# The head of a token model's kernel: K loads of group 0 moved to GpSimd, batch 1's norm moved up, a semaphore per gathered tile, memsets moved to the front

## The chip, the cores and the metric

The kernel runs on one core of one Trainium2 chip. The metric is the device time of one execution in microseconds (us). The engines are TensorE (PE; its weight loads are shown as PEld), VectorE (DVE), ScalarE (ACT), GpSimd (POOL) and SyncE (SP), which only issues DMAs here. Each works through its own instruction stream in order and waits on semaphores.

## The reference

The input is 4 batches of 512 token ids. Three stages follow each other, all in float32 (C = 192 channels).

```python
h = LN(concat_h table_h[(id + 1) * prime_h % 4096]) * scale + bias     # 8 tables of 24 columns
x = layernorm(h)                                                       # attention, 12 heads of 16
q, k, v = split(x @ qkv_w.T + qkv_b)
out = softmax(q k^T / 4) v ; out = out @ proj_w.T + proj_b
u = out / |out| per head ; sim = 10 u u^T, where < 0: -inf
h = h + (softmax(sim) v) @ proj_w.T + proj_b
x = layernorm(h)                                                       # 8 experts, the best 2 of each token
h = h + sum_k weight_k * (gelu(x @ w1[e_k] + b1) @ w2[e_k] + b2)
```

## The kernel before, in words

Tokens lie on the 128 partitions, 16 tiles of 128 tokens in all, four (`CT`) for each of the 4 batches (`B`). GpSimd gathers the 16 tiles of embeddings into `H` by indirect DMAs, one for each tile (line 743), and each batch has one semaphore, `gathered[b]`, that counts its four.

For each batch there follow: `embed_norm` (five parts: statistics, moments and centring on VectorE, `rstd` as a logarithm and an exponential on ScalarE, and `affine` on VectorE, which first refines the root by three small instructions), `attn_stats` (the same statistics once more, on the result, with its own `rstd` on ScalarE), and `attn_norm`, which refines that root and writes the normalised tokens `X`. TensorE transposes `X` (`x_transpose`, line 1515), ScalarE copies that to `XT`, and TensorE makes q, k and a third projection c (`q_proj`, `k_proj`, `c_proj`, line 1526; c holds the q and k of the third group of a batch) and v (`v_proj`, line 1534).

Scores are made in bf16 with float32's accuracy: each of q, k and c is split in three bf16 parts, H, M and L. ScalarE copies H from PSUM (line 889), TensorE subtracts it in PSUM (line 1481), ScalarE copies M (line 861), TensorE subtracts it, and ScalarE copies L (line 864). SyncE and GpSimd then copy the parts by DMA into stacks of 96 rows, `QS` and `KS`, so that one matmul of 96 rows adds six products of parts (`load_part`, line 627; the DMA is on line 634, and in the trace `KS` of the first pass is named late_stacks, all else of the kind arena). There are 12 groups, three for each batch, of four heads; a group needs six Q copies and six K copies of 64 KB. SyncE issues all Q copies; it also issues the K copies of group 0, alternating with the Q copies (lines 687 to 691). GpSimd issues the K copies of all other groups. Before ScalarE overwrites the parts of q, k or c with the next batch's, it waits until all copies of them have landed (`wait_stack`, line 637).

A group goes through 16 units of scores for its row maxima (`max_unit`: TensorE line 1542, VectorE reduces each, line 1258), then 16 units of exponentials (`exp_unit`: TensorE line 1550, ScalarE line 908; two rows more of the stack hold minus the maximum, and ones on K's side), products with v (line 1470), and a second pass of the same form on the similarity of the outputs (line 1557). Last comes the routing and the expert layer (lines 1607 to 1650), which works on the slots of tokens in a loop of its own.

The order of the work is one list, `EVENTS`: `schedule` makes the events of each kind in order, and `PLACE` gives each kind its places in the list. Every engine runs through the same list and takes what is its own. So a place decides between which of its other instructions an engine does the work; PSUM banks come from the string `BANKS` in the order of the units that need one. Around the head, the list before is:

```text
0-6   batch 0: stats, moments, centre, rstd, affine, attn stats, attn moments     7  batch 1: stats
8, 9  batch 0: attn rstd, attn_norm     10, 11 x_transpose 0     12 q_proj 0     13 load 0
14    batch 1: moments     15 k_proj 0     16 load 1     17 mid q     18, 19 loads 2, 3     20 batch 1: centre
21, 22 loads 4, 5     23 batch 1: rstd     24 low q     25 mid k     26-28 batch 1: affine, attn stats, attn moments
29    batch 2: stats     30 batch 1: attn rstd     31 v_proj 0 (first half)     32, 34 loads of group 1     33 low k
35    batch 1: attn_norm     36-38 batch 2: moments, centre, rstd     39 c_proj 0     40, 41 x_transpose 1
42    v_proj 0 (second half)     43 mid c     44 ... max_unit
```

GpSimd's stream begins with the identity matrix, the 16 gathers, four memsets of ones into `KS` (line 749; two rows of each of the four stacks), and the constants of the routing (lines 752 to 771). Only then come its loads. VectorE clears the two accumulators in PSUM and sets the ones columns of `V` right after `attn_norm` of batch 0 (lines 1247 to 1251).

## Time and profile before

| what | us |
|---|---|
| median of 3 runs (567.55 to 568.56) | 568.02 |
| the profiled execution | 566.18 |
| its span in the trace | 564.4 |
| TensorE busy | 513.6 (91%) |
| VectorE busy | 402.0 (71%) |
| ScalarE busy | 351.3 (62%) |
| GpSimd busy | 204.8 (36%) |

The span is the trace's own length, from the first instruction to the last; the profiled execution's time has 1.8 us around it. Mean granted clock of TensorE is 0.981 of full speed. The busy time of an engine counts its work, not its DMA issues' waits; a row "SPq" or "POOLq" is the queue that issues. In the chain of waits each step is followed back to what released it, so its shares tell on what the end hangs.

### The profile page before, as it was taken

To read this page: it belongs to the slowest core of one execution; us is meant where nothing else is said; L and a number is where in the kernel's file an instruction comes from. 1 tells how busy PE (TensorE), PEld (TensorE's weight loads), DVE (VectorE), ACT (ScalarE), POOL (GpSimd) and SP (SyncE) were. 2 spreads that over 40 slices of the span, in tenths; PEclk is the share of its full clock that TensorE was granted. 3 is DMA by queue.
4 is the path that set the end of the run, shared out by engine and by line. 5 is a ranking of instruction groups with operands and counts; after the bars stand their busy time and mean duration, and the time that the engine had idled before them with its cause. 6 is when DMAs were issued, how large, how long until landed. Compare 5 with 4: busy or idle time off the path is not lost.

```text
span 564.4 us, 11981 instructions
## 1 busy us (share of the span) xinstructions
PE 513.6 (91%) x3542; PEld 322.7 (57%) x3543; DVE 402.0 (71%) x895; ACT 351.3 (62%) x830; POOL 204.8 (36%) x260
## 2 busy tenths in 40 slices
PE   0469999999999999999999999689989999999990
PEld 0244334543353433545364443479979999999990
DVE  2659999898989999998579999477764343443420
ACT  1134796788898888989989989353323344243330
POOL 6873040235042140102221220223555666666542
PEclk9989999999999999999999999889999999999996
DMA  6266051348061241104334469792232333333322
GB/s 118 63 110 88 29 101 15 57 65 130 33 104 43 64 85 48 58 1 122 57 58 112 67 177 277 206 323 47 42 49 45 57 60 49 49 50 55 41 29 21
DMA packets 42539, 45.23 MB, mean 80 GB/s; under 512 B 10419, under 2 KB 37429, under 8 KB 42486
## 3 DMA queue, kind: packets, MB, share of 16 engines
q0 software_dynamic: 12672, 19.58, 20.2%
q1 hardware_dynamic: 29814, 25.01, 18.8%
q8 instruction: 26, 0.43, 0.4%
q14 instruction: 27, 0.22, 0.2%
HBM read 17.88 MB, written 7.70 MB: 45 GB/s over the span
## 4 chain that ended last, share of the span: by engine, by line
PE 79%; issue 7%; DVE 5%; ACT 4%; DMA 2%; DVEq 1%; POOL 0%; POOLq 0%; SPq 0%; ACTq 0%
PE psum L1470 15%; PE psum L1630 12%; PE psum L1550 8%; PE psum L1607 8%; PE psum L1542 7%; PE psum L1557 7%; PE psum L1614 4%; PE psum L1579 4%; PE psum L1526 3%; PE psum L1515 3%; PE psum L1568 2%; PE psum L1534 2%; DMA result<-T,slot_dest 2%; ACT arena L908 1%; PE psum L1481 1%
## 5 line engine op out<-in xcount | busy, mean ns | idle before, releaser
L908 ACT ACTIVATE arena<-psum 128x512 f32<-128x512 f32 x384 | 203.6, 630 | 17.2 <-PE psum L1550 8.1
L1258 DVE TENSOR_REDUCE MX<-psum 128x1 f32<-128x512 f32 x192 | 121.2, 682 | 13.3 <-PE psum L1542 12.5
L1272 DVE SCALAR_TENSOR_TENSOR arena<-arena 128x1024 f32<-128x1024 f32 x86 | 101.1, 1217 | 9.0 <-ACT arena L908 8.9
L1470 PE MATMUL psum<-arena 128*17 128x512 f32 x768 | 95.8, 596 | 0.3 <-ACT arena L854 0.2
L802 POOL DMA_INDIRECT result<-T,slot_dest x39 | 65.4, 1676 | 61.3 <-DVE T L1389 59.5
L634 POOL DMA_DIRECT2D KS<-arena x72 | 37.0, 514 | 139.3 <-PE psum L1557 84.5
L941 ACT ACTIVATE arena<-psum,b_sb 128x128 f32<-128x128 f32 x120 | 32.5, 395 | 59.0 <-PE psum L1614 44.5
L634 POOL DMA_DIRECT2D late_stacks<-arena x66 | 34.1, 518 | 84.7 <-PE psum L1550 72.5
L784 POOL DMA_INDIRECT xg_sb<-x_rows,slot_token x39 | 40.8, 1047 | 58.9 <-PE psum L1600 24.3
L1607 PE MATMUL psum<-O,arena 128*128 128x128 f32 x468 | 57.3, 279 | 2.7 <-DVE O L1022 2.0
L1607 PEld LDWEIGHTS psum<-O,arena 128*128 128x128 f32 x468 | 55.7, 195 | 3.8 <-DVE O L1022 3.0
L1557 PE MATMUL psum<-KS,QS 96*128 96x512 bf16 x192 | 56.4, 380 | 0.2
L941 ACT ACTIVATE SQ<-psum,b_sb 128x128 f32<-128x128 f32 x60 | 16.6, 376 | 50.5 <-PE psum L1614 50.5
L1389 DVE TENSOR_SCALAR T<-T,X 128x192 f32<-128x192 f32 x39 | 12.5, 322 | 46.9 <-DMA result<-T,slot_dest 35.5
L1018 DVE COPY arena<-arena 128x1152 f32 x39 | 30.4, 787 | 20.3 <-issue 9.9
L1542 PE MATMUL psum<-late_stacks,arena 96*128 96x512 bf16 x144 | 44.3, 380 | 0.2
L1550 PE MATMUL psum<-arena,late_stacks 98*128 98x512 bf16 x144 | 43.9, 380 | 0.0
L1630 PE MATMUL psum<-arena 128*128 x240 | 41.1, 327 | 0.4 <-issue 0.3
L1470 PEld LDWEIGHTS psum<-arena 128*17 128x17 f32 x768 | 15.6, 96 | 44.3 <-issue 35.5
L1630 PEld LDWEIGHTS psum<-arena 128*128 128x128 f32 x240 | 38.7, 190 | 1.0 <-issue 0.9
L1557 PEld LDWEIGHTS psum<-KS,QS 96*128 96x128 bf16 x192 | 17.1, 98 | 37.2 <-issue 22.9
L1614 PE MATMUL psum<-O,arena 64*128 64x128 f32 x468 | 32.2, 284 | 0.0
(226 smaller groups left out, 741.3 us busy)
## 6 DMA issues: line engine op xcount, KB each, us to landing
QS<-arena SPq DMA_DIRECT2D x72, 64.0 KB, 3.2
KS<-arena POOLq DMA_DIRECT2D x72, 64.0 KB, 3.4
arena<-w SPq DMA_DIRECT2D x8, 576.0 KB
late_stacks<-arena POOLq DMA_DIRECT2D x66, 64.0 KB, 3.6
arena<-arena SPq DMA_DIRECT2D x54, 64.0 KB, 4.1
arena<-w SPq DMA_DIRECT2D x8, 384.0 KB
late_stacks<-arena SPq DMA_DIRECT2D x24, 64.0 KB, 2.6
x_rows<-X SPq DMA_DIRECT2D x4, 384.0 KB, 2.6
```

The costliest lines, as they stand in the source:

```text
L634: eng.dma_start(dst[g % SLOTS[ps]][r * D:(r + 1) * D, :, :].rearrange("d h n -> d (h n)"), part_rows(role, parts[r], g)).then_inc(done[g % ...
L802: pool.indirect_dma_start(out, bass.IndirectOffsetOnAxis(ap=slot_dest[:, j:j + 1], axis=0), Y[j % 2], None, compute_op=ALU.add).then_inc(s ...
L908: act.activation((P1, P2)[ps][:, n % PRING, :], s, ACT.Exp, scale=(QSCALE, SIM_SCALE)[ps]).then_inc(done, 1)
L1258: dve.tensor_reduce(MX[:, g % 2, CT * i + c:CT * i + c + 1], slot(k), AX_X, ALU.max).then_inc(freed[BANK[k]], 1)
L1272: dve.scalar_tensor_tensor(p, p, 1.0, p, ALU.is_ge, ALU.mult).then_inc(masked, 1)
L1470: last = pe.matmul(acc[ps][32 * i:32 * i + VW, :], V[b][:, c, GH * (g % GB) + i, :], (P1, P2)[ps][:, n % PRING, :], start=c == 0, stop=c = ...
L1542: last = pe.matmul(s, QS[0][sl][0:SD, i, c * P:(c + 1) * P], KS[0][sl][0:SD, i, :], start=True, stop=True)
L1550: last = pe.matmul(s, KS[0][sl][:, i, c * P:(c + 1) * P], QS[0][sl][:, i, :], start=True, stop=True)
L1557: last = pe.matmul(s, QS[1][sl][:, i, c * P:(c + 1) * P], KS[1][sl][:, i, :], start=True, stop=True)
L1607: pe.matmul(hid_ps[i][hc], W1S[i][:, hc * P:(hc + 1) * P], XGT[i][:, 0, :], start=hc % HB == 0, stop=False, skip_group_check=True)
L1614: last = pe.matmul(hid_ps[i][HB * h + m], W1S[i][half, HID + m * P:HID + (m + 1) * P], XGT[i][half, 1, :], start=False, stop=True, skip_gr ...
L1630: last = pe.matmul(y_ps[i], HT[r][:, hc, :], w2_sb[:, bass.ds(e, 1), hc, :].rearrange("p o d -> p (o d)"), start=hc == 0, stop=hc == HC - 1)
```

## The change

Five things are done, all of them in the head or for it.

1. `PLACE`: the norm of batch 1 is moved up on VectorE and ScalarE. All its parts but `attn_norm` now lie between places 9 and 20, `stats` behind batch 0's `attn_norm` instead of ahead of its root, and both of its `rstd` ahead of `k_proj`. q, k, their mid and low parts and the loads of group 0 have later numbers, but their order among each other is as before. From place 30 on nothing is moved but `stats` of batch 2 (29 to 30).
2. The K loads of group 0 are issued by GpSimd, and count on the same semaphore as the others (`first_k_loaded` is gone). For that GpSimd's constants of the routing and the memset of the fourth stack move behind the K loads of group 2. The memsets of the other three stacks stay where they were.
3. The first load of group 1, on SyncE and on GpSimd, waits until the L parts of q and k of batch 0 are written.
4. The tiles of batch 0 have a semaphore each, and the first statistics wait for one tile at a time.
5. The memsets of the accumulators and of `V` come right behind VectorE's first constants. TensorE waits for a stack's ones at its group's first exponential, for as many stacks as that group needs, instead of for all four at group 0's.

In the diff, the body of `routing_constants` is that of the block removed, line by line.

```diff
--- before.py
+++ after.py
@@ -161,40 +161,40 @@
 
 PLACE = {
     ('embed_norm', 'stats'): (
-        0, 7, 29, 212),
+        0, 9, 30, 212),
     ('embed_norm', 'moments'): (
-        1, 14, 36, 214),
+        1, 12, 36, 214),
     ('embed_norm', 'centre'): (
-        2, 20, 37, 219),
+        2, 14, 37, 219),
     ('embed_norm', 'rstd'): (
-        3, 23, 38, 232),
+        3, 13, 38, 232),
     ('embed_norm', 'affine'): (
-        4, 26, 142, 234),
+        4, 15, 142, 234),
     ('attn_stats', 'stats'): (
-        5, 27, 152, 239),
+        5, 18, 152, 239),
     ('attn_stats', 'moments'): (
-        6, 28, 168, 332),
+        6, 19, 168, 332),
     ('attn_stats', 'rstd'): (
-        8, 30, 181, 377),
+        7, 20, 181, 377),
     ('attn_norm',): (
-        9, 35, 182, 381),
+        8, 35, 182, 381),
     ('x_transpose',): (
         10, 11, 40, 41, 195, 199, 397, 403),
     ('q_proj',): (
-        12, 58, 213, 429),
+        16, 58, 213, 429),
     ('load_qk',): (
-        13, 16, 18, 19, 21, 22, 32, 34, 47, 54, 67, 68, 69, 70, 72, 73, 74, 75, 84, 85, 86, 112, 121, 122, 145, 146,
+        17, 22, 24, 25, 26, 27, 32, 34, 47, 54, 67, 68, 69, 70, 72, 73, 74, 75, 84, 85, 86, 112, 121, 122, 145, 146,
         158, 161, 162, 177, 178, 179, 196, 198, 207, 208, 228, 229, 230, 262, 264, 270, 287, 288, 292, 293, 295, 318,
         358, 359, 360, 366, 402, 404, 450, 451, 452, 523, 524, 534, 543, 551, 552, 568, 569, 575, 611, 632, 719, 726,
         727, 728),
     ('k_proj',): (
-        15, 64, 233, 455),
+        21, 64, 233, 455),
     ('mid', 'q_proj'): (
-        17, 71, 220, 435),
+        23, 71, 220, 435),
     ('low', 'q_proj'): (
-        24, 80, 231, 449),
+        28, 80, 231, 449),
     ('mid', 'k_proj'): (
-        25, 77, 241, 462),
+        29, 77, 241, 462),
     ('v_proj',): (
         31, 42, 52, 96, 205, 272, 477, 594),
     ('low', 'k_proj'): (
@@ -561,6 +561,7 @@
         ident_set, consts_set, ones_set, stack_ones_set, rows_ready = (
             sem(x) for x in ("ident_set", "consts_set", "ones_set", "stack_ones_set", "rows_ready"))
         gathered = [sem(f"gathered{b}") for b in range(B)]
+        first_gathered = [sem(f"first_gathered{c}") for c in range(CT)]
         filled = [sem(f"psum_filled{s}") for s in range(BANKS_IN_RING)]
         freed = [sem(f"psum_freed{s}") for s in range(BANKS_IN_RING)]
         hi_written, mid_written, lo_written, row_hi = (sem(x) for x in ("hi_written", "mid_written", "lo_written", "row_hi"))
@@ -568,7 +569,6 @@
         pool_step = sem("pool_step")
 
         qk_loaded = {x: [sem(f"{x}_loaded{s}") for s in range(SLOTS[0])] for x in "qk"}
-        first_k_loaded = sem("first_k_loaded")
         row_loaded = [sem(f"row_loaded{s}") for s in range(SLOTS[0])]
         sim_loaded = {x: [sem(f"sim_{x}_loaded{s}") for s in range(SLOTS[1])] for x in "qk"}
         pv_done = [sem("pv1_done"), sem("pv2_done")]
@@ -627,6 +627,8 @@
         def load_part(eng, g, r, ps, dst, role, parts, done):
 
             n = SPLIT[split_source(role, g)]
+            if (g, r, ps) == (1, (K_ORDER if role == "K" else Q_ORDER)[0], 0):
+                eng.wait_ge(lo_written, max(SPLIT[(kind, (0,))] for kind in ("q_proj", "k_proj")) + 1)
             eng.wait_ge({"H": hi_written, "M": mid_written, "L": lo_written}[parts[r]], n + 1)
             last_reader = ("exp_unit", "sim_unit")[ps]
             if g >= SLOTS[ps]:
@@ -636,11 +638,7 @@
 
         def wait_stack(e, side, g):
 
-            if side == "k" and g == 0:
-                e.wait_ge(first_k_loaded, LOADS)
-            else:
-                own_first = side == "k" and g % SLOTS[0] == 0
-                e.wait_ge(qk_loaded[side][g % SLOTS[0]], LOADS * (g // SLOTS[0] + 1 - own_first))
+            e.wait_ge(qk_loaded[side][g % SLOTS[0]], LOADS * (g // SLOTS[0] + 1))
 
         def wait_past(e, s_, v):
 
@@ -687,8 +685,6 @@
                     if kind == "load_qk":
                         g, r = args
                         load_part(sp, g, Q_ORDER[r], 0, QS[0], "Q", Q_PARTS, qk_loaded["q"])
-                        if g == 0:
-                            load_part(sp, g, K_ORDER[r], 0, KS[0], "K", K_PARTS, [first_k_loaded])
                     elif kind == "max_row":
                         g, = args
                         wait_consumed(sp, unit("max_row", g))
@@ -742,37 +738,45 @@
                 for t in range(TILES):
                     pool.indirect_dma_start(H[:, t, :], None, table,
                                             bass.IndirectOffsetOnAxis(ap=rows_sb[:, t:t + 1], axis=0)
-                                            ).then_inc(gathered[t // CT], 16)
-
-                pool.wait_ge(ident_set, 1)
-                for n in range(SLOTS[0]):
+                                            ).then_inc(gathered[t // CT] if t >= CT else first_gathered[t], 16)
+
+                def stack_ones(n):
+
                     pool.memset(KS[0][n][SD:SD + 2, :, :], 1.0).then_inc(stack_ones_set, 1)
                     pool.wait_ge(stack_ones_set, n + 1)
 
...
+                def routing_constants():
+
...
+                for n in range(SLOTS[0] - 1):
+                    stack_ones(n)
                 for kind, args in EVENTS:
-                    if kind == "load_qk" and args[0] > 0:
+                    if kind == "load_qk":
                         load_part(pool, args[0], K_ORDER[args[1]], 0, KS[0], "K", K_PARTS, qk_loaded["k"])
+                        if args == (GB - 1, len(K_PARTS) - 1):
+                            stack_ones(SLOTS[0] - 1)
+                            routing_constants()
                     elif kind == "load_sim":
                         load_part(pool, args[0], K_ORDER[args[1]], 1, KS[1], "T", K_PARTS, sim_loaded["k"])
 
@@ -980,10 +984,12 @@
                     chain_at[name] = steps[0]
                     ins.then_inc(dve_step, 1)
 
-                def norm_part(name, part, mean_var, src, done):
+                def norm_part(name, part, mean_var, src, done, landed=None):
 
                     if part == "stats":
                         for c in range(CT):
+                            if landed is not None:
+                                dve.wait_ge(landed[c], 16)
                             last = dve.bn_stats(stats[name][:, c, :], src[:, c, :])
                         chain(name, last)
                     elif part == "moments":
@@ -1010,6 +1016,11 @@
                 dve.tensor_scalar(rows_sb[:, :], ids_sb[:, :], BUCKETS - 1, None, ALU.bitwise_and).then_inc(rows_ready, 1)
                 dve.memset(XT[KW:KW + 1, 0, :], 1.0)
                 dve.memset(OT[KW:KW + 1, 0, :], 1.0).then_inc(consts_set, 1)
+                dve.memset(acc[0], 0.0)
+                dve.memset(acc[1], 0.0)
+                for n in range(B):
+                    last = dve.memset(V[n][:, :, :, D:VW], 1.0)
+                last.then_inc(ones_set, 1)
 
                 def stage(j, i):
 
@@ -1207,8 +1218,8 @@
                         tiles = slice(CT * b, CT * (b + 1))
                         h, moments, rstd = H[:, tiles, :], mv_x[:, tiles, :], rstd_x[:, tiles]
                         if part == "stats":
-                            dve.wait_ge(gathered[b], 16 * CT)
                             if b >= 1:
+                                dve.wait_ge(gathered[b], 16 * CT)
                                 dve.wait_ge(in_moments, 2 * b)
                         if part == "centre":
                             dve.wait_ge(in_moments, 2 * b + 1)
@@ -1226,7 +1237,7 @@
                                                                 ALU.mult, ALU.add)
                             chain("in", last)
                         elif part != "rstd":
-                            norm_part("in", part, moments, h, in_moments)
+                            norm_part("in", part, moments, h, in_moments, None if b else first_gathered)
                     elif kind == "attn_stats":
                         b, part = args
                         tiles = slice(CT * b, CT * (b + 1))
@@ -1242,13 +1253,6 @@
                         if b >= 1:
                             wait_filled(dve, unit("x_transpose", b - 1, 1))
                         norm_apply(X, H[:, tiles, :], mv_x[:, tiles, :], rstd_x[:, tiles]).then_inc(x_ready, 1)
-                        if b == 0:
-
-                            dve.memset(acc[0], 0.0)
-                            dve.memset(acc[1], 0.0)
-                            for n in range(B):
-                                last = dve.memset(V[n][:, :, :, D:VW], 1.0)
-                            last.then_inc(ones_set, 1)
                     elif kind == "max_unit":
                         g, q, j = args
                         i, c = (2 * q + j) % GH, q // 2
@@ -1543,8 +1547,8 @@
                     elif kind == "exp_unit":
                         g, q, j = args
                         i, c, sl = (2 * q + j) % GH, q // 2, g % SLOTS[0]
-                        if (g, q, j) == (0, 0, 0):
-                            pe.wait_ge(stack_ones_set, SLOTS[0])
+                        if (q, j) == (0, 0) and g < SLOTS[0]:
+                            pe.wait_ge(stack_ones_set, g + 1)
                         if (q, j) == (0, 0):
                             pe.wait_ge(row_loaded[sl], 32 * (g // SLOTS[0] + 1))
                         last = pe.matmul(s, KS[0][sl][:, i, c * P:(c + 1) * P], QS[0][sl][:, i, :], start=True, stop=True)
```

## Rows read from the trace of the kernel before

**Rows 1.** The chain of waits of the whole span: shares by engine.
```profile
PE 79%; issue 7%; DVE 5%; ACT 4%; DMA 2%; DVEq 1%; POOL 0%; POOLq 0%; SPq 0%; ACTq 0%
```

**Rows 2.** Busy time by stretch: from:to, length, busy of each engine, granted clock, DMA share, GB/s.
```profile
41.60:53.00 11.40, 11.11 (x42) 4.76 (x41) 10.90 (x19) 5.45 (x12) 2.57 (x6) 1.00 0.73 80
53.00:290.00 237.00, 237.00 (x1428) 101.96 (x1427) 211.94 (x372) 206.14 (x425) 53.60 (x105) 1.00 0.32 63
```

**Rows 3.** The chain in order of time, 0 to 80 us: start, length, what.
```profile
44.84 5.64 DMA arena<-arena
```

**Rows 4.** The timeline, VectorE and ScalarE, 11 to 21 us: start, length, instructions [idle before].
```profile
11.22 1.14 DVE L987 BATCH_NORM_STATS2 stats_in<-H 128x6 f32<-128x192 f32 x4 [7.14 <-DMA H<-table,rows_sb]
12.40 0.38 DVE L992 BATCH_NORM_AGGREGATE mv_x<-stats_in 128x2 f32<-128x6 f32 x4
...
17.88 1.14 DVE L987 BATCH_NORM_STATS2 stats_in<-H 128x6 f32<-128x192 f32 x4
18.14 0.20 ACT L819 ACTIVATE rstd_x<-log_in 128x4 f32<-128x4 f32 x1
...
18.93 0.15 DVE L997 SCALAR_TENSOR_TENSOR log_in<-rstd_x 128x4 f32<-128x4 f32 x1
...
19.51 1.29 DVE L1003 TENSOR_SCALAR X<-H,mv_x,rstd_x 128x192 f32<-128x192 f32 x4
...
20.91 0.48 DVE L1247 MEMSET psum<- 128x512 f32 x1
```

**Rows 5.** The timeline of GpSimd, 24 to 54 us: memsets, group 1's and group 3's loads.
```profile
24.23 7.37 POOL L749 MEMSET late_stacks<- 2x2048 bf16 x4
...
34.53 3.17 POOL L634 DMA_DIRECT2D late_stacks<-arena  x6
...
51.96 1.52 POOL L634 DMA_DIRECT2D late_stacks<-arena  x3 [6.49 <-ACT arena L889]
```

**Rows 6.** The timeline of ScalarE and SP, 27 to 46 us.
```profile
27.39 0.60 ACT L889 ACTIVATE arena<-psum 128x512 bf16<-128x512 f32 x1 [3.89 <-PE psum L1526]
...
29.27 0.60 ACT L889 ACTIVATE arena<-psum 128x512 bf16<-128x512 f32 x1 [1.28 <-PE psum L1526]
...
34.42 0.30 ACT L816 ACTIVATE log_in<-mv_x,eps_norm 128x4 f32<-128x4 f32 x1 [2.51 <-DVE mv_x L992]
...
35.23 0.59 ACT L864 ACTIVATE arena<-psum 128x512 bf16<-128x512 f32 x1
...
36.89 8.54 SPq L634 DMA_DIRECT2D arena<-arena  x12
```

**Rows 7.** The timeline of TensorE, VectorE and ScalarE, 32 to 53 us.
```profile
32.37 1.88 PE L1526 MATMUL psum<-arena 97*128 97x512 f32 x4
...
37.52 1.67 PE L1515 MATMUL psum<-ident,X 128*96 128x128 f32 x8 [3.26 <-DVE X L1003]
...
42.02 11.03 DVE L1258 TENSOR_REDUCE MX<-psum 128x1 f32<-128x512 f32 x18 [2.91 <-PE psum L1542]
...
50.58 1.09 ACT L889 ACTIVATE arena<-psum 128x512 bf16<-128x512 f32 x2 [4.72 <-DMA arena<-arena]
...
51.23 0.39 PE L1481 MATMUL psum<-arena,minus_ident 128*128 128x512 bf16 x1
```

**Rows 8.** Busy time by stretch, 28 to 50 us, columns as in rows 2.
```profile
28.00:36.00 8.00, 5.30 (x19) 2.59 (x17) 4.85 (x22) 3.93 (x10) 7.88 (x21) 1.00 0.24 81
36.00:42.00 6.00, 4.48 (x19) 3.96 (x19) 3.03 (x13) 1.35 (x4) 3.23 (x7) 0.72 1.06 145
42.00:48.00 6.00, 5.81 (x24) 2.98 (x24) 5.99 (x10) 2.67 (x6) 1.53 (x3) 1.00 1.15 124
48.00:50.00 2.00, 2.00 (x8) 0.87 (x7) 1.92 (x5) 0.00 (x0) 0.00 (x0) 1.00 0.50 50
```

**Rows 9.** DMA issues, 28 to 36 us: queue, count, KB each, median us to landing.
```profile
arena<-arena SPq DMA_DIRECT2D x6, 64.0 KB, 2.6
```

**Rows 10.** DMA issues, 36 to 50 us.
```profile
late_stacks<-arena POOLq DMA_DIRECT2D x10, 64.0 KB, 5.0
```

42 lines of the change are left out of this document (21 added, 21 removed).

## The prediction

> **What bounds the kernel now.** I read the chain of waits as shares first: 79% of the chain is TensorE, so nearly everywhere only TensorE's own work sets the end [rows 1]. The stretches say where that isn't so: from 53 to 290 us TensorE is busy for all of 237 us at full clock, and before it VectorE has 10.90 busy of 11.40 us between 41.6 and 53 [rows 2]. So an idle TensorE can be won back in the head alone, and whatever the head gains is carried by a TensorE queue that never runs dry behind it. The chain in order of time shows what the last wait of the head is: a DMA that is under way 5.64 us until 50.48 [rows 3]. That DMA is one of the copies of batch 0's Q parts; ScalarE may not overwrite the parts with batch 1's before all copies of groups 0 to 2 have landed, and sat idle 4.72 us for it [rows 7]. Ahead of it VectorE reduces 18 score tiles without a gap from 42.02, 0.613 us each (11.03 over 18) [rows 7].
> So three times of the head matter: when the first scores can be made (42.02 less the matmul), when the 36 copies of groups 0 to 2 have landed (50.48), and how far the reductions are by then.
>
> **Per-tile semaphore and memsets.** VectorE's first statistics wait for all four gathers and take 1.14 us from 11.22 [rows 4]. With a semaphore per tile three of the four run before the last gather lands: 0.85 us saved, or nothing if the gathers land together; I take 0.85, as they are issued more than a microsecond apart. Batch 1's statistics (17.88, 1.14 us) no longer stand between the moments and the refinement, which began at 18.93 though ScalarE was done at 18.34 [rows 4]: another 0.55. X of batch 0 is ready at 19.51 + 1.29 - 1.40 = 19.40 instead of 20.80. The six memsets (two of 0.48 us on PSUM [rows 4], four small ones, an estimated 0.4 together) go into the 7.14 us in which VectorE waited until 11.22 and cost nothing there; 1.4 us leave the queue ahead of batch 1's moments. TensorE's first matmuls and q's first part come 1.40 earlier; that part is written at 27.39 + 0.60 - 1.40 = 26.6 [rows 6], and the first load follows it at once.
>
> **Batch 1's norm moved up.** Before, ScalarE reached its second root of batch 1 at 34.42 after 2.51 us of waiting, and k's last part, queued behind it, was written only at 35.23 + 0.59 = 35.82 [rows 6]. After, VectorE goes from 19.40: statistics 1.18, moments 0.42, centring 1.41, then the refinement when ScalarE's root is there (its two copies of the transposes end at 22.1, root 0.53: 22.65), 0.6, affine 1.41, statistics 1.18, moments 0.42: 26.3 (durations as batch 0's, [rows 4], 1.41 us for an elementwise pass of four tiles being an estimate from X's 1.29). ScalarE's root then fits between q's first part (ends 26.6) and k's, which can't start before 29.27 - 1.40 = 27.87 [rows 6]: 0.7 us of slack. Behind that ScalarE has no wait on VectorE, and k's last part is written at about 32.0 (v's eight matmuls and the mid and low corrections in the order of before). X of batch 1 is ready after statistics of batch 2 (1.14), 0.6 and 1.29: at 29.3. So TensorE runs through: c's four matmuls (1.88 us, before at 32.37 [rows 7]) from 31.2 to 33.05, the transposes and v's tiles directly behind. Before, these began at 37.52 after 3.26 idle, with the granted clock at 0.72 in the stretch around them against 1.00 before and after [rows 7, 8]; from 37.52 to the first score, some 0.4 ahead of the reduction at 42.02, 4.1 us. At full clock I take 2.4 (bounds 2.0 to 4.1). TensorE is ready for the first score at 35.5.
>
> **K loads of group 0 on GpSimd.** Its 16 gathers end at 24.2, unchanged. Four memsets of the stacks took 7.37 us [rows 5], three now take 5.53: GpSimd is free at 29.76, k's first part is there since about 28.5. Six loads at 0.53 us (3.17 over six [rows 5]) instead of SP's 0.71 (8.54 over 12 [rows 6]); the sixth needs k's last part (32.0) and is issued at 32.4. Landings took 2.6 us while the DMA had room (SP's, up to 36 us [rows 9]) and 5.0 while it was full (GpSimd's, [rows 10]); it is about to be full, and I take the middle, 3.8: 36.2, with 35.0 and 37.4 as bounds. It is the later of the two: first reduction at 36.5, 5.5 us earlier than now. The new wait for k's last part ahead of group 1's loads (SP and GpSimd) ends at 32.0, when SP has been through with its six Q loads for a microsecond, and the DMA then still has group 0's to move: I count nothing for it. The constants (31.60 to 34.53 = 2.9 us) and the fourth memset (1.8) come behind group 2's K loads, which are issued by 39.1: done by 44. Queued behind them are group 3's K loads, issued at 51.96 before, after 6.49 idle [rows 5]: at most they could be wanted at 46, so this costs nothing; with that cover gone, up to 1 us of a load that no score needs for long.
>
> **The 36 copies as a stream.** 64 KB each (65.5 thousand bytes). From 28 to 36 us the DMA moved 81 GB/s x 8 = 9.9 of them; from 36 to 42 145 GB/s, 42 to 48 124 GB/s, with a DMA share over 1, and 50 GB/s in the last two microseconds [rows 8]: 9.9 + 13.3 + 11.4 + 1.5 = 36.1. So it was issue-bound up to 36 and full from there, 0.488 us per copy; data ends at about 48.8, and the landing (50.48) is seen 1.7 later. After the change: a load is moved about 1.6 us after its issue as long as the DMA isn't full (an estimate: 2.6 to the landing [rows 9], less a last microsecond). Q loads at 26.6, 27.2, 27.9, and behind the mid part at 29.0, 29.6, 30.3; K loads from 29.8: six moved by 31.4, and from there both queues keep it full. 30 x 0.488 = 14.6: data ends at 46.0, last landing at 47.7. That is 2.8 us earlier, not 5.5. At 145 GB/s it would be 46.6, at 124 GB/s 49.0.
> Which of the two counts: after 17 reductions VectorE wants the 18th score tile, which stands behind the correction of batch 1's q (51.23 before, directly behind ScalarE's part from 50.58 [rows 7]). Before, VectorE came to it at 42.02 + 17 x 0.613 = 52.44, some 0.7 after the tile was there (an estimate: 50.48 and 1.2 for the part, the correction and the score). After, VectorE comes to it at 46.9, and the tile is there at 48.9: VectorE and TensorE now wait there, about 2 us. **Sum: 2.8 + 0.7 = 3.5 us** gained at that point, and carried to the end.
>
> The profiled execution took 566.18 us (span 564.4), the median shown is 568.02. In the profile's terms 562.7; against the median **564.5 us**.
>
> **Rivals.**
> 1. *The DMA keeps up* (faster than I think). If the 0.488 us per copy came from the bad moment at which they were issued, or the copies land by 46, the gain is the first score's, 5.5, or about 5: 563. For it: up to 36 us the share is 0.24 for 9.9 copies, 8 x 0.24 / 9.9 = 0.19 us each [rows 8]. Against: the share stood over 1 for 12 us with both queues in it.
> 2. *GpSimd's own work is held up by VectorE*, which is now busy from 19.4 to 31 beside the gathers and the memsets. The K loads then start up to 1.3 later, the stream's end moves by 0.8: 565.3, or 2.7 gained. Against: the six loads at 34.53 took 0.53 each though VectorE wrote X beside them (they span 36.12 on) [rows 5].
> The Trainium skill (SBUF — State Buffer, Who interferes with whom) says that a VectorE operation in a two-port mode, tensor_scalar among them, shuts GpSimd out for its whole length, descriptor writing included. By it, X of batch 1 (1.29 us at 28.0) would push the memset or the first K load by that much. The row just named shows no such hold, so I give it little.
> 3. *The gain is given back*: a later wait, unchanged in absolute time, takes it. For it: only that the stretch behind 53 has VectorE at 212 of 237 us too [rows 2], close behind TensorE. Against: 237 us without an idle TensorE. Time 568, within 0.2%.
> 4. *Slower: loads from GpSimd hold the DMA longer than SP's.* Of 36 copies 18 instead of 12 now come from GpSimd. If SP's cost 0.19 each wherever they are, the 12.5 full microseconds, with some 15 from SP and 11 from GpSimd, put 0.88 us on each of GpSimd's. Then 12 x 0.19 + 18 x 0.88 = 18.1 behind 31.4, 49.5, landing 51.2: 0.7 later than now, which eats the 0.7 of reserve, no gain at all. It turns to slower by 0.2% from 0.94 us per copy (landing 52.3); at 1.0 the landing is 53.4 and the time 570.2. Against: the stretch with more of GpSimd's (36 to 42) moved more, 145 against 124 GB/s, than the one with more of SP's [rows 8].
>
> **Chances.** Forecast (2.2 to 4.6 gained) 0.54; rival 1 0.17; rival 2 0.09 (gain 1.2 to 2.7 taken with it); rival 3 0.11; rival 4 0.09, of which 0.05 slower by over 0.2%. About 0.2% (1.1 us) is what a measurement of this kernel can tell from no change. That makes 0.81 faster, 0.13 same, 0.06 slower. The forecast's own range is 563.4 to 565.8; for 8 in 10 it has to take in most of rivals 1 and 2 and the edge of no change: 562.3 to 567.2.
>
> **What would show it.** X of batch 0 finished at 19.4, of batch 1 at 29.3; ScalarE's last part of k at 32.0; GpSimd's first load at 29.8; the first reduction at 36.5; ScalarE's first part of batch 1's q still released by a DMA, at 47.8; no half clock between 33 and 36; 36 copies moved from 27 to 46. I am wrong if reductions start after 38, if that part is released by TensorE instead of a DMA (rival 1), if it starts after 50.5 (rival 4), or if TensorE shows new idle time behind 53 (rival 3).

## The result, and the profile after

The changed kernel takes 566.32 us (median of 22 runs, 562.05 to 568.14) against 567.85 of the kernel before beside it: a ratio of 0.9963, 95% interval 0.9946 to 0.9979. It is faster by 0.37%, and that can be told from no change. In two later sessions, each on another chip and beside runs of the kernel before, it took 562.80 (8 runs; 0.9905, 0.9871 to 0.9939) and 563.71 us (12 runs; 0.9944, 0.9920 to 0.9969). Forecast were 564.5 us and a gain of 3.5; the three medians lie 1.5, 5.1 and 4.4 us under those beside them. Why the gain differs by session is the main question below. Medians and ratios here are over fast runs, which leaves out one run of b2_filled (776.42 us at a mean granted clock of 0.659).

The profiled execution of the first session took 568.14 us, the longest of its 22 runs and longer than the one of before (566.18, under that kernel's median), and yet its head is ahead nearly everywhere until the last step. The timeline of VectorE, GpSimd, SP, ScalarE and TensorE in it (start, length, instructions, idle before and who ended it) answers to [rows 4 to 7]:

```profile
10.32 1.24 DVE L993 BATCH_NORM_STATS2 stats_in<-H 128x6 f32<-128x192 f32 x4 [4.59 <-DMA H<-table,rows_sb]
...
18.11 1.25 DVE L1009 TENSOR_SCALAR X<-H,mv_x,rstd_x 128x192 f32<-128x192 f32 x4
...
22.15 6.65 PE L1530 MATMUL psum<-arena 97*128 97x512 f32 x8 [0.73 <-issue]
...
25.94 0.60 ACT L893 ACTIVATE arena<-psum 128x512 bf16<-128x512 f32 x1 [3.46 <-PE psum L1530]
26.43 0.29 ACT L820 ACTIVATE log_in<-mv_x,eps_norm 128x4 f32<-128x4 f32 x1
...
28.83 0.60 ACT L893 ACTIVATE arena<-psum 128x512 bf16<-128x512 f32 x1 [1.88 <-PE psum L1530]
...
30.10 2.70 POOL L636 DMA_DIRECT2D late_stacks<-arena  x5 [0.54 <-POOL late_stacks L745]
...
32.31 0.59 ACT L868 ACTIVATE arena<-psum 128x512 bf16<-128x512 f32 x1
...
33.66 1.04 PE L1519 MATMUL psum<-ident,X 128*96 128x128 f32 x8
...
37.77 10.25 DVE L1262 TENSOR_REDUCE MX<-psum 128x1 f32<-128x512 f32 x17 [5.50 <-PE psum L1546]
...
48.59 1.09 ACT L893 ACTIVATE arena<-psum 128x512 bf16<-128x512 f32 x2 [7.38 <-DMA arena<-arena]
49.25 0.61 PE L1485 MATMUL psum<-arena,minus_ident 128*128 128x512 bf16 x1 [2.34 <-ACT arena L893]
...
50.32 0.69 DVE L1262 TENSOR_REDUCE MX<-psum 128x1 f32<-128x512 f32 x1 [2.30 <-PE psum L1546]
...
53.70 2.76 PE L1530 MATMUL psum<-arena 97*128 97x512 f32 x4
...
58.90 0.38 PE L1554 MATMUL psum<-arena,late_stacks 98*128 98x512 bf16 x1
```

X of batch 0 is finished at 19.36, q's first part at 26.54, k's last part at 32.90 (35.82 before). TensorE goes from c (ends 33.8) straight into the transposes of batch 1, at full speed (1.04 us for 8, before 1.67 after 3.26 idle). The first reduction comes at 37.77, 4.25 earlier. Then comes the new wait: ScalarE waits 7.38 us, to 48.59, for the landing of the Q copies, TensorE 2.34 behind it, and VectorE, which had no gap before, 2.30. And what follows goes at half speed: four matmuls of a projection of batch 1 take 2.76 us at 53.70, where the same four took 1.98 before (at 53.90). The first exponential's matmul, a fixed point that all kernels here share, starts at 58.90. Before, it started at 58.31.

The stretches of the same execution (columns as in [rows 2]) show the rest, and answer to [rows 2, 8]:

```profile
28.00:36.00 8.00, 7.04 (x35) 4.64 (x33) 4.23 (x12) 4.14 (x9) 7.00 (x12) 1.00 0.64 115
36.00:42.00 6.00, 4.87 (x23) 2.67 (x22) 4.23 (x8) 3.03 (x6) 5.21 (x9) 1.00 1.15 137
42.00:46.00 4.00, 3.85 (x12) 1.45 (x12) 4.00 (x8) 0.00 (x0) 3.26 (x17) 1.00 1.16 130
46.00:48.00 2.00, 0.91 (x4) 0.10 (x1) 2.00 (x4) 0.00 (x0) 0.00 (x0) 1.00 0.45 41
48.00:50.00 2.00, 0.75 (x2) 0.23 (x3) 0.02 (x1) 1.20 (x3) 0.03 (x1) 0.66 0.00 0
50.00:55.00 5.00, 5.00 (x12) 2.16 (x11) 3.90 (x7) 2.32 (x5) 3.04 (x6) 0.50 0.33 100
53.00:290.00 237.00, 237.00 (x1423) 101.66 (x1421) 210.34 (x368) 204.71 (x422) 51.35 (x101) 0.99 0.31 62
```

The DMA is full from 36 to 46 at 137 and 130 GB/s, as before at 145 and 124, only earlier. TensorE did nothing from 46.9 to 49.25; its granted clock fell to half within that time, at about 48.6 (the mean of 48 to 50 is 0.66), and stayed there to about 55.5. From 58.9 on the loss of 0.6 us is carried on unchanged: one and the same matmuls of the last group come at 343.59 before and 344.18 after.

### The profile page after: what moved, and what is told of

Read it like the earlier page. It is cut to its first block, busy times and chain, and to the rows that moved or that the text cites. A ratio compares the mean times of both kernels' runs of the same rounds, so it can differ in the third digit from the quotient of the medians.

```text
span 566.4 us, 11984 instructions
## 1 busy us (share of the span) xinstructions
PE 515.3 (91%) x3542; PEld 322.3 (57%) x3543; DVE 404.2 (71%) x895; ACT 351.5 (62%) x830; POOL 206.1 (36%) x266
## 4 chain that ended last, share of the span: by engine, by line
PE 71%; DMA 9%; DVE 7%; issue 5%; ACT 3%; DVEq 2%; SPq 1%; POOLq 0%; POOL 0%; ACTq 0%
PE psum L1474 15%; PE psum L1554 8%; PE psum L1634 8%; PE psum L1546 7%; PE psum L1561 7%; DMA result<-T,slot_dest 6%; PE psum L1611 6%; PE psum L1530 4%; PE psum L1583 3%; PE psum L1618 3%; PE psum L1519 2%; PE psum L1572 2%; PE psum L1485 2%; ACT arena L912 1%; DMA arena<-arena 1%
## 5 line engine op out<-in xcount | busy, mean ns | idle before, releaser
L636 POOL DMA_DIRECT2D late_stacks<-arena x72 | 37.0, 516 | 82.3 <-PE psum L1554 74.4
L1611 PE MATMUL psum<-O,arena 128*128 128x128 f32 x468 | 59.0, 284 | 2.7 <-DVE O L1033 2.0
L788 POOL DMA_INDIRECT xg_sb<-x_rows,slot_token x39 | 39.6, 1016 | 59.8 <-PE psum L1604 24.9
L1611 PEld LDWEIGHTS psum<-O,arena 128*128 128x128 f32 x468 | 57.4, 200 | 3.8 <-DVE O L1033 2.9
L1561 PEld LDWEIGHTS psum<-KS,QS 96*128 96x128 bf16 x192 | 17.1, 98 | 37.2 <-issue 22.9
L1384 DVE TENSOR_TENSOR T<-psum,arena 128x192 f32<-128x192 f32 x39 | 13.8, 355 | 26.4 <-PE psum L1634 15.9
```

Of the source, the lines that this page charges most:

```text
L636: eng.dma_start(dst[g % SLOTS[ps]][r * D:(r + 1) * D, :, :].rearrange("d h n -> d (h n)"), part_rows(role, parts[r], g)).then_inc(done[g % ...
L1561: last = pe.matmul(s, QS[1][sl][:, i, c * P:(c + 1) * P], KS[1][sl][:, i, :], start=True, stop=True)
L1611: pe.matmul(hid_ps[i][hc], W1S[i][:, hc * P:(hc + 1) * P], XGT[i][:, 0, :], start=hc % HB == 0, stop=False, skip_group_check=True)
```

## The experiments

Two times sum up each kernel's head in its profiled execution. Behind the first reduction the reductions set the pace, behind ScalarE's H part of batch 1's q ("q part") the corrections and what waits for them. The last column but one is the start of the first exponential's matmul, and the last tells which execution was profiled.

| kernel | first reduction | q part, released by | first exponential | that execution's us |
|---|---|---|---|---|
| before | 42.02 | 50.58, DMA | 58.31 | 566.18 |
| changed, first | 37.77 | 48.59, DMA | 58.90 | 568.14 |
| changed, a1_again | 36.84 | 46.93, DMA | 54.63 | 562.54 |
| changed, b1_again | 37.43 | 47.97, DMA | 55.67 | 563.73 |
| a2_narrow_wait | 37.07 | 42.61, TensorE | 53.19 | 558.94 |
| b3_narrow_wait | 36.64 | 42.18, TensorE | 52.77 | 557.93 |
| a3_filled | 36.63 | 47.33, DMA | 55.03 | 562.84 |
| b2_filled | 37.30 | 48.33, DMA | 56.03 | 562.73 |
| a4_k_on_sp | 40.99 | 49.15, DMA | 58.27 | 566.95 |
| b4_norm_alone | 40.68 | 50.07, DMA | 57.98 | 566.72 |
| c1_before_narrow | 43.30 | 50.17, TensorE | 60.53 | 569.55 |
| c2_small_parts | 42.25 | 50.79, DMA | 59.85 | 569.04 |
| c3_without_norm | 41.10 | 49.05, DMA | 57.40 | 566.52 |
| c4_warm_narrow | 34.54 | 41.40, TensorE | 51.76 | 556.64 |

**The changed kernel again (a1_again, b1_again).** Nothing edited.

> The changed kernel once more, nothing edited. Theory (the head's gain is lost to a wait for the 36 copies and to the half clock that follows it): the profile shows again ScalarE's first part of batch 1's q released by a DMA at 48.6 us (within 0.5), TensorE idle about 2.3 us before it, the granted clock at 0.5 from about 48.5 to 55 us, and the first exponential's matmul at 58.9. Rival (the half clock was an accident of one execution): the wait is there again, the clock stays at 1.00, and the first exponential's matmul comes at 56 to 57. Time about 0.3% under the kernel before.

> The changed kernel a third time. In one execution the head held half clock from 48.5 to 55.5 us and the first exponential's matmul came at 58.90, in another the clock stayed at 1.00 and it came at 54.63. Theory (an idle TensorE of 1.5 to 2.5 us ahead of batch 1's q makes the clock fall in some executions and not in others, about 3 us each time): times in two clumps, about 562.5 with mean clock 0.986 or more and 566 to 567.5 with 0.983 or less. Rival (two chips differ): all on one side.

In neither profile did the clock fall in the head. The same stretches of a1_again:

```profile
46.00:48.00 2.00, 0.42 (x2) 0.11 (x2) 1.10 (x2) 1.07 (x2) 0.00 (x0) 1.00 0.00 0
48.00:50.00 2.00, 1.90 (x9) 0.74 (x9) 1.42 (x3) 2.00 (x6) 1.69 (x4) 1.00 0.17 55
50.00:55.00 5.00, 5.00 (x22) 2.83 (x21) 5.00 (x10) 1.55 (x4) 1.36 (x3) 1.00 0.38 116
```

and its wait and what follows it:

```profile
46.93 1.08 ACT L893 ACTIVATE arena<-psum 128x512 bf16<-128x512 f32 x2 [6.65 <-DMA arena<-arena]
47.58 0.39 PE L1485 MATMUL psum<-arena,minus_ident 128*128 128x512 bf16 x1 [1.60 <-ACT arena L893]
...
50.24 1.95 PE L1530 MATMUL psum<-arena 97*128 97x512 f32 x4
...
54.63 0.38 PE L1554 MATMUL psum<-arena,late_stacks 98*128 98x512 bf16 x1
```

So the wait for the DMA is there each time, and the half clock only in one of three, behind idle times of TensorE of 2.34 us (it fell), 1.60 and 2.05 us (it didn't). From the q part to the first exponential it is 54.63 - 46.93 = 7.70 us, in b1_again 7.70 too, and in the first profile 58.90 - 48.59 = 10.31: the half clock costs 2.61 us. The rival was right that it comes by execution, and its numbers (56 to 57) were too late since the copies landed earlier. The times of single executions: over 564.5 us are 19 of 22 in the first session, 2 of 8 and 5 of 12 in the others, all with a mean clock of 0.983 or less, and of the sixteen under it all but two (563.46 and 563.58 us) have 0.986 or more. I expected two clumps and see more of a slope. The rival of two chips that differ asked for all runs on one side; both later sessions have runs on both, so it is out as stated, but it isn't on record on which chip the first session ran, and a difference there isn't ruled out.

**The narrower wait (a2_narrow_wait, b3_narrow_wait).**

```diff
                                 for g in range(max(0, GB * b - SLOTS[0]), GB * b):
-                                    wait_stack(act, side, g)
+                                    if (g % GB == 2) == (kind == "c_proj"):
+                                        wait_stack(act, side, g)
```

The third group of a batch is made from c's parts, so q's and k's parts may be overwritten before its copies have landed.

> The changed kernel, but ScalarE waits before it overwrites q's and k's parts only for the copies of groups that are made from those parts (groups 0 and 1 of a batch), and before c's for group 2's. Theory: the wait falls away, since group 1's copies land by about 43; reductions run without a gap from 37.8, the clock stays at 1.00, the first exponential's matmul comes at 54.1 (58.31 before, less the 4.2 us by which reductions start earlier), and the time is 4.2 us under the kernel before, 0.7%. Rival (the copies are not the limit, the gain is lost elsewhere in the head): first exponential at 57 or later, time as the changed kernel's, 0.3% under before.

> The changed kernel with the narrower wait ahead of q's and k's parts. Theory: no idle TensorE between 38 and 60 us, so the first exponential's matmul at 53 to 54 and a time of 560 whatever the changed kernel does beside it: 1.3% under the kernel before. Rival (what it gained on the first chip was chance of the clock): no more than 1 us under the changed kernel.

It took 559.88 us (0.9866, 0.9824 to 0.9909) and 559.47 (0.9878, 0.9836 to 0.9921), 2.9 and 4.2 us under the changed kernel beside it and 8.0 and 8.6 under the kernel before, where I had expected 4.2 and then 7.5. In a2_narrow_wait ScalarE is now released by TensorE, and the reductions have no gap:

```profile
37.07 10.86 DVE L1263 TENSOR_REDUCE MX<-psum 128x1 f32<-128x512 f32 x18 [4.91 <-PE psum L1547]
...
42.61 0.60 ACT L894 ACTIVATE arena<-psum 128x512 bf16<-128x512 f32 x1 [2.09 <-PE psum L1531]
...
53.19 0.38 PE L1555 MATMUL psum<-arena,late_stacks 98*128 98x512 bf16 x1
```

That shows the wait as the place where the gain stopped. From the first reduction to the first exponential it is 16.12 us here and 16.13 in b3_narrow_wait: this is the head's length when the reductions alone set the pace.

The head gives 1.44 us of the gain in a2_narrow_wait (54.63 - 53.19) and 2.90 in b3_narrow_wait (55.67 - 52.77). The edit narrows the wait of every batch, and some 0.5 us more comes from the later ones: from the first exponential to sixteen of the last products with v (343.59 before) it is 285.28 us in the kernel before and in all three profiles of the changed kernel, 284.78 and 284.83 here. What is left lies behind that point, where a1_again and b1_again take 220.9 and 221.0 us with 6.8 us at half clock between 355 and 385, and these two 219.2 and 218.5 with 3.4; that may be chance of the execution.

These runs also put a limit on what the mean clock can tell. Eight of the twelve took 557.93 to 560.55 us at 0.986 or more, four 563.16 to 564.48 at 0.980 or 0.981. So times split here too, by some 4 us, though the wait for the copies is gone: a low mean clock doesn't say that it was lost in the head.

**TensorE kept busy at the wait (a3_filled, b2_filled).** It computes 12 products more that nobody uses.

```diff
+                        if kind == "mid" and args == ("q_proj", 1):
+                            pe.wait_ge(zeros_set, 1)
+                            pe.wait_ge(ones_set, 1)
+                            nought = zeros[:, :].bitcast(BF16)
+                            for _ in range(12):
+                                pe.matmul(acc[1][:, 0:2 * C], nought[:, 0:P], nought, start=True, stop=True, skip_group_check=True)
```

> The changed kernel with 12 matmuls of zeros (384 columns bf16, about 0.16 us each, 2 us together) on TensorE just ahead of its wait for batch 1's q; they write zeros where zeros are. Theory: the copies still land at 48.5 and ScalarE's part of q starts at 48.6, but TensorE isn't idle before it, so the clock stays at 1.00; the first exponential's matmul comes at 56.3 instead of 58.9, and the time is some 2 us under the kernel before (0.4%) with less spread. Rival (the clock doesn't matter there, VectorE sets the pace): first exponential at 58.5 to 59.

> The changed kernel with the 12 matmuls of zeros ahead of its wait for batch 1's q. If the clock falls there in the changed kernel's executions beside it, theory: here it stays at 1.00 between 46 and 56 us, the first exponential's matmul comes at 55 to 56, and the median is 562.8 or 2 us and more under the changed kernel's; if the clock doesn't fall there beside it, both medians are the same within 0.5 us. Rival (the clock falls for another reason): half clock around 50 us here too.

562.84 us (0.9905, 0.9865 to 0.9945) and 562.73 (0.9905, 0.9873 to 0.9938), beside 562.80 and 563.71 of the changed kernel. TensorE was idle for 0.26 and 0.59 us ahead of the q part's correction. The clock stayed at 1.00 in both, and the 7.70 us behind the q part are there again (55.03 - 47.33, 56.03 - 48.33). But it stayed at 1.00 in the changed kernel's executions beside them too, so this doesn't settle that the idle makes it fall. One of its 12 runs was over 564.5 us (566.82), of the changed kernel's 20 beside them 7: a hint and no more.

**K loads back on SP (a4_k_on_sp).**

```diff
                         load_part(sp, g, Q_ORDER[r], 0, QS[0], "Q", Q_PARTS, qk_loaded["q"])
+                        if g == 0:
+                            load_part(sp, g, K_ORDER[r], 0, KS[0], "K", K_PARTS, [first_k_loaded])
...
-                    if kind == "load_qk":
+                    if kind == "load_qk" and args[0] > 0:
```

> The changed kernel, but the K loads of group 0 are issued by SP in turn with the Q loads, as before the change; GpSimd's other loads, its memsets and constants stay as in the changed kernel. Theory (the copies are one stream with one rate whoever issues them): first reduction at 36.5 to 37.8, ScalarE's part of batch 1's q at 48.6 within 0.7. Rival (a copy issued by GpSimd holds the DMA 0.9 us, one by SP 0.2): 12 instead of 18 of them end the stream some 4 us earlier, ScalarE's part of q comes by 45 or is released by TensorE, and the time is 0.7% under before.

567.33 us (0.9983, 0.9961 to 1.0006): nearly all of the gain is gone. The q part came at 49.15, so the stream's end moved 0.6 to 2.2 us later with 12 instead of 18 copies from GpSimd, where the rival had it 4 us earlier; the rival of a costly GpSimd copy is refuted. From 38 to 46 us the DMA moved 129 GB/s. But the first reduction, which I expected at 37.8 at the latest, came at 40.99:

```profile
35.31 0.59 SPq L637 DMA_DIRECT2D late_stacks<-arena  x1
...
40.37 1.01 PE L1553 MATMUL psum<-late_stacks,arena 96*128 96x512 bf16 x2 [4.65 <-DMA late_stacks<-arena]
```

SP issues its twelfth load of group 0 at 35.31, while GpSimd has been issuing group 1's since 33.05, so the last K copy lands in a full DMA. TensorE is idle 4.65 us for it, its granted clock falls at about 37.5 in that time, and it works at 0.50 until 44.4:

```profile
38.00:42.00 4.00, 1.63 (x4) 0.58 (x5) 1.01 (x2) 0.00 (x0) 0.85 (x2) 0.50 1.14 133
```

**The parts alone (b4_norm_alone, c3_without_norm, c2_small_parts).** The first is the kernel before with the new places (the first hunk of the change) and nothing else; the second the changed kernel with the old places; the third the kernel before with the tile semaphores and VectorE's memsets moved (the hunks of `first_gathered`, `norm_part` and the memsets).

> The kernel before with the new places alone (batch 1's norm moved up); SP still issues group 0's K loads, GpSimd's memsets and constants, the gather semaphores and VectorE's memsets stay as before. Theory: k's last part is written at 33 to 34 instead of 35.8, but SP's 12 loads in turn end no sooner than 36 to 37 as before, so the first reduction comes at 40 to 41 (42.02 before), with TensorE idle and at half clock ahead of it; 566.5 to 568, same as before. Rival (the norm is what counts): first reduction at 37 to 38 and the changed kernel's time.

> The changed kernel with the places of before: all parts of the change but the norm of batch 1 moved up. Theory: k's last part waits again for batch 1's second root on ScalarE and is written at 34 to 34.5 instead of 32.9, X of batch 1 comes at 35 to 36 instead of 30, TensorE makes the second half of v after it: first reduction at 40 to 41, at half clock ahead of it; 0.1 to 0.3% under before. Rival (GpSimd's K loads alone carry the gain): first reduction at 38, and the changed kernel's time.

> The kernel before with the semaphore per gathered tile and VectorE's memsets at the front alone. Theory: X of batch 0 is finished 0.8 us earlier (20.0), first reduction 0.8 to 1.5 us earlier since batch 1's norm, the SP loads and k's last part all follow it: 40.5 to 41.3; time 0.15% under before, not told from no change. Rival: nothing moves, since another wait comes last.

The norm alone: 567.44 us (0.9993, 0.9971 to 1.0015), first reduction 40.68, as expected (the half clock came behind it, from 41.4 to 44.9, not ahead). All but the norm: 566.06 (0.9959, 0.9933 to 0.9985), first reduction 41.10, k's last part at 34.90; this is 0.4% faster and can be told from no change, more than the 0.1 to 0.3% expected. The small parts alone: 566.58 (0.9971, 0.9940 to 1.0002), no verdict; the transposes of batch 0 began at 20.14 instead of 20.95, as expected, but its first reduction came at 42.25, not 41. The projections behind the transposes took 6.85 us there against 5.63 before, which took the start back, and the execution held half clock from 39.4 to 46.3. So in that session the small parts with GpSimd's K loads gave 1.7 us, of which the small parts alone gave 1.2, and the K loads' share of 0.5 can't be told from nothing. The norm without them gave 0.6, and all but the K loads (a4_k_on_sp) 0.5, where the whole change gave 5.1 beside it. The norm and GpSimd's K loads thus need each other: with the norm alone the loads of SP are late (TensorE waits 3.88 us for a K copy), with the loads alone TensorE's queue stands before the transposes of batch 1 (3.26 us for X).

**The narrower wait in the kernel before (c1_before_narrow).** The same edit as above.

> The kernel before with the narrower wait ahead of q's and k's parts alone. Theory: in the kernel before the reductions set the pace up to 52 us and the wait for the copies ended just in time, so the part of batch 1's q is made earlier (44 to 47 us instead of 50.58) and nothing follows: first exponential's matmul at 57.5 to 58.3, time as before within 0.1%. Rival (that wait cost time in the kernel before too): first exponential at 56 or earlier, 0.3% and more under before.

567.02 us (0.9969, 0.9937 to 1.0002): no verdict. Its profiled execution, of 569.55 us, doesn't test the expectation: it held half clock from 39.7 to 46.6, the first reduction came at 43.30, and the q part, now released by TensorE, at 50.17, not at 44 to 47. By the two lengths above, though, the kernel before can be judged from its own profile: 42.02 + 16.13 = 58.15 by the reductions, 50.58 + 7.70 = 58.28 by the q part, measured 58.31. Both ended together, the wait by 0.13 us last. The same two lengths, the later of them, give 57.77 for 57.98 in b4_norm_alone and 57.23 for 57.40 in c3_without_norm; where the reductions ran at half clock for a time and set the pace (a4_k_on_sp, c1_before_narrow, c2_small_parts, c4_warm_narrow), the first exponential came 1.1 to 1.4 us later than both.

**A better version (c4_warm_narrow).** The narrower wait, and:

```diff
+                pe.wait_ge(clips_set, 2)
+                pe.wait_ge(in_rstd, 1)
+                for _ in range(64):
+                    pe.matmul(psum[:, 5, 0:P], minus_ident[:, :], minus_ident[:, :], start=True, stop=True, skip_group_check=True)
...
-                for n in range(SLOTS[0] - 1):
-                    stack_ones(n)
...
+                        if args[0] < GB and args[1] == len(K_PARTS) - 1:
+                            stack_ones(args[0])
```

with batch 1's `attn_stats` `rstd` at place 28 instead of 20, and `k_proj`, the loads, mid q and low q one place earlier each.

> Towards a better version: the changed kernel with the narrower wait; 64 small matmuls into an unused PSUM bank from ScalarE's first root (12.6 us) on, so that TensorE isn't idle before its first transposes at 19.5; the memset of each stack's ones behind that group's K loads instead of ahead of all; and batch 1's second root on ScalarE behind k_proj and q's low part. Theory: the first transposes and projections run at full clock, 1.9 + 6.6 us become 1.0 + 3.5, q's first part is written at 23.6 and k's at 25.2 instead of 26.6 and 29.4, the K loads begin there, first reduction at 33 to 34, first exponential's matmul at 49 to 50, and 556 to 557 us, 2% under before. Rival (the DMA, not the parts, sets the first reduction): no earlier than 35.5, and no more than 1.5 us under the version with the narrower wait alone (559.7).

556.87 us, 0.9800 (0.9757 to 0.9844): 2% under the kernel before, and the fastest here. It is 3.0 and 2.6 us under the narrower wait alone, though of another session, where the rival allowed 1.5; what each of its other edits gives wasn't measured apart.

```profile
12.48 6.27 PE L1440 MATMUL psum<-minus_ident 128*128 128x128 bf16 x64 [12.48 <-ACT rstd_x L823]
19.18 1.08 PE L1524 MATMUL psum<-ident,X 128*96 128x128 f32 x8 [0.43 <-DVE X L1010]
21.04 3.68 PE L1535 MATMUL psum<-arena 97*128 97x512 f32 x8 [0.78 <-ACT arena L880]
...
34.12 1.99 PE L1551 MATMUL psum<-late_stacks,arena 96*128 96x512 bf16 x6 [1.68 <-DMA late_stacks<-arena]
```

The projections take 3.68 us instead of 6.65 in the first profile of the changed kernel (6.02 and 6.16 in the others). The first reduction, at 34.54, is half a microsecond later than expected, and the first exponential at 51.76 two: I had counted no more than 16 us behind the reduction and too early a start, and here TensorE, idle 1.68 us for the last K copy, is at half clock once more (mean granted clock 0.61 from 34 to 38 us). By the reductions' length it would be 34.54 + 16.13 = 50.67.

## Why the prediction was right, and where it was off

- *The time.* 566.32 us lies in the stated 562.3 to 567.2, but outside the forecast's own 563.4 to 565.8, and the first session's gain of 1.5 us is one that the prediction gave to rival 2. Rival 2's cause didn't occur: GpSimd's three memsets took 1.80 us each and its K loads began at 30.10, 30.19 and 29.87 against 29.8 forecast. So that hit is in part luck. The mechanism is what held: of the 3.5 us forecast at the first exponential 3.68 and 2.64 were measured in two profiles, and in the third the clock took them.
- *The order of the steps.* X of batch 0: forecast 19.40, measured 19.36. q's first part: 26.6, 26.54. The per-tile semaphore saved what was counted (0.80 us for 0.85), though it is seen differently: the statistics began at 10.32 and ended at 11.56 instead of 12.36. The memsets cost nothing at the front.
- *k's parts.* Forecast 27.87 for the start of k's H part, measured 28.83, 27.89 and 28.60 in the three profiles: the eight matmuls of q and k took 6.65, 6.02 and 6.16 us, 5.63 before. c's take 0.47 each (1.88 for four), at full speed. I had them full as early as before, shifted with the work; in the first profile the rise came later. There the last part was written at 32.90, not 32.0, and the sixth K load issued at 33.2.
- *First reduction.* Forecast 36.5; 37.77, 36.84 and 37.43 in the three profiles: a gain of 4.3 to 5.2 instead of 5.5. In the first, the sixth K load was issued at 33.2 instead of 32.4, behind k's later part, and TensorE was released by its landing at 37.35. GpSimd's memsets set the start of the K loads, as forecast: the first load came 0.54, 0.30 and 0.35 us behind the third memset, when k's first part had been written (29.43, 28.48, 29.20). They didn't set the first reduction in the first profile, where the sixth load waited 0.40 us for k's last part.
- *The stream of copies* was the right bound. Forecast: last landing seen by ScalarE at 47.8; measured 48.59, 46.93, 47.97, in each "released by DMA". The rate (137 and 130 GB/s) came as worked out (0.488 us for 64 KB is 134), and the data, forecast to end at 46.0, ended just before 46 in a1_again, before 47 in b1_again and between 47 and 48 in the first. In a4_k_on_sp, with 12 copies from GpSimd, the rate was the same 129. Rival 1 (the DMA keeps up) and rival 4 (GpSimd's copies cost more) are out, and so is rival 3 (a later wait takes the gain back): TensorE is busy for all of 237 us from 53 to 290 as before.
- *The step that failed is "2.8 + 0.7".* The 0.7 us of reserve were there for VectorE's 18th tile (it comes 1.30 us behind the q part in a1_again and b1_again, so 51.88 before, and VectorE came to it at 52.44), but not for the first exponential. That hangs on TensorE's path from the q part through the corrections and the next projection, which starts 3.3 us behind the q part before and after (53.90, 50.24, 51.28) and passes VectorE's reserve by. I worked with the moment at which the 18th tile was ready, where only the whole path counts: 7.70 us from the q part to the first exponential in four profiles (a1_again, b1_again, a3_filled, b2_filled), and 7.73 before. The kernel before hung on both paths at once, so the gain is that of the q part alone: 50.58 - 47.97 = 2.61, and 58.31 - 55.67 = 2.64 was measured in b1_again; 3.65 and 3.68 in a1_again.
- *What I left out is the clock behind the new wait.* I wrote that TensorE and VectorE would wait there for about 2 us (measured 2.34 and 2.30), and didn't ask what TensorE's clock does behind an idle time of that length, though [rows 7, 8] show it falling behind 3.26 us of it. In the first profile it fell. By the q part's 1.99 us alone the first exponential would have come at 58.31 - 1.99 = 56.32; with the half clock's 2.61 it came at 58.90. In all, the first profile has 22.9 us at half clock, a1_again 15.4 and b1_again 15.7, so the 6.9 us in the head are nearly the whole difference. That the first session gained only 1.5 us because most of its runs lost the clock in the head is argued from this one profile and the mean clocks, not shown for each run; the narrower wait's runs split in the same way without such a wait, and nothing here shows that the idle time is what makes the clock fall.
- *Carried to the end* held: 0.59 us of difference at 58.9 and the same 0.59 at 344. Behind that, single executions differ by some 3 us of their own: from the first exponential to the end of the span it is 506.1 us before, 507.5, 506.2 and 506.3 in the changed kernel.
- Why two sessions gave more (4.4 and 5.1 us) than the head's 2.6 and 3.7 against the profile of before stays open in part. That profile is of an execution of 566.18, under the median; executions with the same head order in c1_before_narrow and c2_small_parts (569.55 and 569.04 us) held half clock for 6.9 us, to 46.6 and 46.3, and reached the first exponential at 60.53 and 59.85. In three profiles of three the old head shows half clock somewhere between 38 and 46 (for 3.4 us in before), and no profile of the changed kernel does. That the kernel before often loses more there than in its profile would explain the sessions; it wasn't measured on the kernel before itself.

## What to carry to other kernels

When a step is made earlier, follow each queue to the next thing that doesn't move with it; here it was a stream of copies at a fixed rate, and the wait for it was wider than the data needed, so narrowing the wait gave 2.9 and 4.2 us more, beside the change's 5.1 and 4.4. A reserve at one step (0.6 us at VectorE's 18th tile) is none for a step that hangs on another path: measure a path from one fixed point to the next, not from an estimate of when one tile is ready. And a wait of about two microseconds on a TensorE that was busy was followed by half clock in one execution of three, which cost 2.61 us more than the wait; compare several executions before you explain one.

## What the runs showed of the hardware

GpSimd's memset held a VectorE instruction. In the first profile of the changed kernel VectorE's first tile of X of batch 1 started at 27.82, beside the third memset of the stacks (1.80 us from 27.76), and took 1.86 us; the others took 0.37 each:

```profile
24.04 5.51 POOL L745 MEMSET late_stacks<- 2x2048 bf16 x3
...
27.82 1.86 DVE L1009 TENSOR_SCALAR X<-H,mv_x,rstd_x 128x192 f32<-128x192 f32 x1
```

It was so in each profile of the changed kernel: the longest tile took 1.86, 1.94 and 1.56 us, and it ended 0.12 us behind the memset each time. In a1_again the first tile, started at 27.50 in the second memset, was held too (0.65 us), and the second, started at 28.07, beside the third. It was not so in c4_warm_narrow, where no memset ran beside them (0.37 to 0.38 each). The rule of the Trainium skill that I had weighed (SBUF — State Buffer, Who interferes with whom: whoever issues first holds the shared pair for the whole instruction) fits, for the instruction held ends with the memset, but with the roles exchanged: I had asked what VectorE does to GpSimd's loads, and it was GpSimd that came first. VectorE's other operations in that time, the statistics and the scalar_tensor_tensor passes (1.14 and 1.40 us for four tiles), were not held. X of batch 1 came at 30.5 instead of 29.3, behind which c's matmuls hid it.

The first work of TensorE in an execution of these kernels starts at about half speed, and the column of the granted clock doesn't show it. From 24 to 26 us it reads 1.00, before and in the changed kernel, while the eight matmuls of the projections take 5.63 us before and 6.65 in the changed kernel's first profile, against some 3.7 at full speed. The rise comes at another time in each execution: the trace's first record of the clock, which says 1.00, is at 25.74 in b3_narrow_wait, 26.57 in a1_again, 27.42 in b1_again and 28.14 in the first, 3.7 to 6.0 us behind the projections' start, and they take 5.48, 6.02, 6.16 and 6.65 us: half a microsecond more for each one that the record comes later. With 64 small matmuls (6.27 us in all) ahead of it, the same work, transposes and projections, took 1.08 and 3.68 us instead of 1.91 and 6.65.
